# Both FiLM products in one run of matmuls, their 64-row parts in the two row halves of the array, biases added by GpSimd and VectorE

## What is computed

```
Q = x @ Wq ; K = ctx @ Wk                      # 4 heads of 32, 257 context rows of 192
attn = softmax over the 32 largest scores of each row, mean over the heads
c_t  = (attn_mean @ (ctx @ Wv)) * text_mask
x'   = layernorm(x, g_norm_in, b_norm_in)
scale_in, shift_in   = split(c_t @ W_film_in + b_film_in)
x'   = x' * (1 + mod_gate * scale_in) + mod_gate * shift_in
y    = s4d(x')                                 # a causal convolution over the 32 tokens, plus x' * D_skip
scale_out, shift_out = split(c_t @ W_film_out + b_film_out)
y    = y * (1 + mod_gate * scale_out) + mod_gate * shift_out
xt   = x + y ;  xt = xt + gelu(layernorm(xt) @ W1 + b1) @ W2 + b2 ;  layernorm(xt)
```

## Time and profile before

| | |
|---|---|
| median of 3 runs | 705.63 us (705.25 to 710.68) |
| the profiled execution | 706.75 us, its span 705.0 us |
| PE matmul busy | 609.8 us, 87% of the span |
| DVE busy | 524.6 us, 74% |
| ACT busy | 318.5 us, 45% |
| POOL busy | 223.4 us, 32% |

### The profile page before, as it was taken

One profiled execution on the slowest core, in us unless ns is written; L12 is line 12 of the kernel. 1 busy time (PEld: TensorE's weight loads), 2 busy tenths in 40 slices (PEclk: granted clock), 3 DMA queues, 4 the chain that ended last, 5 costly groups with the idle time before them and its releaser, 6 DMA issues.

```text
span 705.0 us, 13818 instructions
## 1 busy us (share of the span) xinstructions
PE 609.8 (87%) x4082; PEld 456.9 (65%) x4082; DVE 524.6 (74%) x1817; ACT 318.5 (45%) x795; POOL 223.4 (32%) x580
## 2 busy tenths in 40 slices
PE   0368377889999999989998999899989999998776
PEld 0134134668787878767877787778777878775665
DVE  5579948486969697968787878788877878885332
ACT  6441011435555555535554555455535454544512
POOL 2540301224242424242524242424242515242420
PEclk9969567999999999999999999999999999999977
DMA  5394040112020303021211212020202030000000
GB/s 161 79 327 134 25 167 24 55 43 75 23 92 14 98 7 104 2 63 42 63 40 32 72 37 66 9 96 8 95 9 96 8 95 9 1 8 1 9 7 8
DMA packets 18462, 40.61 MB, mean 58 GB/s; under 512 B 4741, under 2 KB 11222, under 8 KB 17896
## 3 DMA queue, kind: packets, MB, share of 16 engines
q1 hardware_dynamic: 18408, 40.03, 17.8%
HBM read 37.85 MB, written 2.16 MB: 57 GB/s over the span
## 4 chain that ended last, share of the span: by engine, by line
PE 51%; DVE 30%; issue 10%; ACT 2%; DMA 2%; DVEq 1%; POOL 1%; SPq 1%; POOLq 0%; ACTq 0%
PE D L1067 9%; PE B L1067 6%; PE B L1090 5%; DVE work L835 4%; PE D L1084 4%; PE B L1156 4%; DVE top L829 3%; PE S L1043 3%; PE S L1059 2%; PE S L1060 2%; PE B L1144 2%; PE B L1145 2%; PE PA L1129 2%; DVE ang L862 2%; DVE work L815 2%
## 5 line engine op out<-in xcount | busy, mean ns | idle before, releaser
L485 POOL TENSOR_SCALAR var_in<-mv 128x1 f32<-128x1 f32 x64 | 13.3, 207 | 298.8 <-DVE mv L951 161.8
L835 DVE MATCH_REPLACE8 work<-top,work 128x257 f32<-128x257 f32 x192 | 77.3, 411 | 0.0
L1084 PE MATMUL D<-expw,ang 128*128 128x256 f32 x256 | 71.8, 406 | 5.2 <-ACT ang L550 2.8
L1067 PE MATMUL D<-ang,e_w 128*128 128x128 f32 x512 | 72.5, 289 | 0.0
L829 DVE MAX8 top<-work 128x8 f32<-128x257 f32 x192 | 71.7, 415 | 0.4 <-ACT kern_f L545 0.4
L1067 PEld LDWEIGHTS D<-ang,e_w 128*128 128x128 f32 x512 | 64.5, 199 | 10.1 <-issue 10.1
L1067 PEld LDWEIGHTS B<-ang,w 128*128 128x128 f32 x512 | 60.5, 194 | 7.9 <-issue 6.3
L1067 PE MATMUL B<-ang,w 128*128 128x128 f32 x512 | 60.8, 278 | 0.0
L1090 PE MATMUL B<-expw,ang 128*128 128x256 f32 x256 | 57.9, 379 | 0.0
L1084 PEld LDWEIGHTS D<-expw,ang 128*128 128x128 f32 x256 | 46.5, 196 | 15.9 <-DVE ang L858 6.2
L1090 PEld LDWEIGHTS B<-expw,ang 128*128 128x128 f32 x256 | 47.4, 190 | 5.8
(11 more groups left out here) (244 smaller groups left out, 1277.9 us busy)
## 6 DMA issues: line engine op xcount, KB each, us to landing
ctx_n<-in_ctx_n SPq DMA_DIRECT2D x16, 768.0 KB
ctx_t<-in_ctxT SPq DMA_DIRECT2D x16, 514.0 KB
ctx_t<-in_ctxT SPq DMA_DIRECT2D x16, 257.0 KB
x_all<-in_x SPq DMA_DIRECT2D x4, 512.0 KB, 5.8
out<-out_sb SPq DMA_DIRECT2D x16, 128.0 KB, 1.7
ctx_l<-in_ctx_l SPq DMA_DIRECT2D x64, 24.0 KB
w<-in_W SPq DMA_DIRECT2D x1, 1024.0 KB
e_w<-in_e_w SPq DMA_DIRECT2D x1, 1024.0 KB, 4.8
```

The lines of the kernel that those rows point to most:

```text
L835: V.match_replace(work[:, 2 * q + k, :], top[:, 2 * q + k, 8 * r8:8 * r8 + 8], work[:, 2 * q + k, :], TAKEN).then_inc(chains["taken"], 1)
L1067: ins = MM(bank[:, 128 * m:128 * m + 128], w[:, k, at:at + 128], xs[:, 128 * k:128 * k + 128], start=k == 0, stop=k == 1)
L1084: MM(bank, act2[:, k, :], e_w2[:, k, :], start=True, stop=True).then_inc(s["eo_mm"], 1)
```

## The change

PE computes both ways in one run, ahead of `xf`. `zT2` now has 128 rows: ACT copies the 64-row transpose twice, to rows 0 to 63 and to rows 64 to 127. `film2` is 128 x 512: rows 0 to 63 hold the way in, rows 64 to 127 the way out. The two 64-row matmuls stand one behind the other, in the two row halves of the array, into different banks. The bias row is gone; biases are spread over 128 partitions in `film_b`. For the way in, POOL makes `x_bias = xhat * bias_scale + bias_shift` and DVE adds it to `xf` in a third instruction; for the way out, ACT copies bank B1 to `film_o`, POOL adds the bias, and DVE reads `film_o` in place of the bank. Since the forward transform writes B1, PE waits for that copy (`film_a`). Some semaphores of DVE are joined (`best` into `logit`, `rsd` into `pg`, `pn` into `rsc`) with the same waits.

```diff
@@ loads
-                (brow[64:65, 0:2 * D], d["b_film_in"], "ld_film"), (brow[64:65, 2 * D:4 * D], d["b_film_out"], "ld_film"),
+                (brow[:, 0:2 * D], d["b_film_in"].broadcast_to([128, 2 * D]), "ld_film"), (brow[:, 2 * D:4 * D], d["b_film_out"].broadcast_to([128, 2 * D]), "ld_film"),
@@ GpSimd, step
                 if b:
                     weights(b, 1)
+                if b:
+                    wait_apart(pool, chains["xhat"], b.count(1, 1), passed_g)
+                    wait_apart(pool, s["xf_v"], b.count(1, 0), passed_g)
+                    nc.gpsimd.tensor_tensor(x_bias[:, :], xhat[b.p][:, :], film_b[:, 0:D], ALU.mult).then_inc(chains["xbias"], 1)
+                    wait_apart(pool, chains["xbias"], b.count(1, 1), passed_g)
+                    nc.gpsimd.tensor_tensor(x_bias[:, :], x_bias[:, :], film_b[:, D:2 * D], ALU.add).then_inc(s["xb0_g"], 1)
                 if a:
...
                     norm(2, c)
                 if b:
+                    wait_apart(pool, s["film_a"], b.count(1, 1), passed_g)
+                    nc.gpsimd.tensor_tensor(film_o[:, :], film_o[:, :], film_b[:, 2 * D:4 * D], ALU.add).then_inc(s["film_g"], 1)
                     norm(0, b)
@@ ScalarE, step
                     A(zT1[:, :], PA[:, 256:384], ACT.Copy)
-                    A(zT2[0:64, :], PA[0:64, 384:512], ACT.Copy).then_inc(s["zT_a"], 1)
+                    A(zT2[0:64, :], PA[0:64, 384:512], ACT.Copy)
+                    A(zT2[64:128, :], PA[0:64, 384:512], ACT.Copy).then_inc(s["zT_a"], 1)
+                if b:
+                    wait(act, s["y_mm"], one(b))
+                    wait(act, s["xt_v"], b.count(1, 0))
+                    copy(film_o[:, :], B1[:, :], "film_a")
@@ VectorE, step
                     V.tensor_tensor(xf[:, :], xhat[b.p][:, :], B0[:, 0:D], ALU.mult).then_inc(chains["xf"], 1)
...
-                    V.tensor_tensor(xf[:, :], xf[:, :], B0[:, D:2 * D], ALU.add).then_inc(s["xf_v"], 1)
+                    V.tensor_tensor(xf[:, :], xf[:, :], B0[:, D:2 * D], ALU.add).then_inc(chains["xf"], 1)
+                    wait(dve, chains["xf"], b.count(2, 2))
+                    wait(dve, s["xb0_g"], one(b))
+                    V.tensor_tensor(xf[:, :], xf[:, :], x_bias[:, :], ALU.add).then_inc(s["xf_v"], 1)
...
-                    wait(dve, s["y_mm"], one(b))
-                    V.tensor_tensor(yb[:, :], yb[:, :], B1[:, 0:D], ALU.mult).then_inc(chains["yb"], 1)
+                    wait(dve, s["film_g"], one(b))
+                    V.tensor_tensor(yb[:, :], yb[:, :], film_o[:, 0:D], ALU.mult).then_inc(chains["yb"], 1)
@@ TensorE, step
                     wait(pe, s["gb_a"], b.count(1, 0))
+                    wait(pe, s["xt2_v"], b.count(1, 0))
                     MM(B0[:, :], zT1[:, :], film1[:, 0:512], start=True, stop=False)
-                    MM(B0[:, :], zT2[:, :], film2[:, 0:512], start=False, stop=True).then_inc(s["fin_mm"], 1)
+                    MM(B0[:, :], zT2[0:64, :], film2[0:64, :], start=False, stop=True).then_inc(s["fin_mm"], 1)
+                    MM(B1[:, :], zT2[64:128, :], film2[64:128, :], start=True, stop=False)
+                    MM(B1[:, :], zT1[:, :], film1[:, 512:1024], start=False, stop=True).then_inc(s["y_mm"], 1)
...
                     wait(pe, s["xf_v"], one(b))
-                    wait(pe, s["xt2_v"], b.count(1, 0))
+                    wait(pe, s["film_a"], one(b))
...
-                    MM(B1[:, :], zT1[:, :], film1[:, 512:1024], start=True, stop=False)
-                    MM(B1[:, :], zT2[:, :], film2[:, 512:1024], start=False, stop=True).then_inc(s["y_mm"], 1)
```

More of the change, by code:

```diff
@@ L175, in build @@
         zT1 = sb("zT1", [128, 128])
-        zT2 = sb("zT2", [65, 128])
+        zT2 = sb("zT2", [128, 128])
+        film_o = sb("film_o", [128, 2 * D])
+        x_bias = sb("x_bias", [128, D])
         xf = over("ang", D)
@@ L284, in build @@
         s = {n: sem(n) for n in names}
-        chains = {n: sem("self_" + n) for n in "tm g0 g1 g2 g3 len bn0 bn1 bn2 bn3 top taken u xhat xf logit best pg rsd yb rsc pn pT".split()}
+        chains = {n: sem("self_" + n) for n in "tm xbias g0 g1 g2 g3 len bn0 bn1 bn2 bn3 top taken u xhat xf logit pg yb rsc pT".split()}
         passed_v, passed_g = sem("passed_v"), sem("passed_g")
@@ L887, in step @@
                     V.scalar_tensor_tensor(logit[:, :], dots[:, NE:2 * NE], inorm[:, :], dots[:, 0:NE], ALU.mult, ALU.add).then_inc(chains["logit"], 1)
-                    wait_apart(dve, chains["logit"], one(dd), passed_v)
-                    V.max(best[:, :], logit[:, :]).then_inc(chains["best"], 1)
+                    wait_apart(dve, chains["logit"], dd.count(2, 1), passed_v)
+                    V.max(best[:, :], logit[:, :]).then_inc(chains["logit"], 1)
                 if b:
@@ L897, in step @@
                 if dd:
-                    wait(dve, chains["best"], one(dd))
+                    wait(dve, chains["logit"], dd.count(2, 2))
                     V.tensor_scalar(nbest[:, :], best[:, 0:1], -1.0, None, ALU.mult).then_inc(s["nbest_v"], 1)
@@ L911, in step @@
                     V.scalar_tensor_tensor(pg[:, :], logit[:, :], best[:, 1:2], e_d[:, :], ALU.is_ge, ALU.mult, accum_out=sum_d[:, :]).then_inc(chains["pg"], 1)
-                    wait(dve, chains["pg"], one(dd))
-                    V.reciprocal(rsum_d[:, :], sum_d[:, :]).then_inc(chains["rsd"], 1)
-                    wait(dve, chains["rsd"], one(dd))
+                    wait(dve, chains["pg"], dd.count(2, 1))
+                    V.reciprocal(rsum_d[:, :], sum_d[:, :]).then_inc(chains["pg"], 1)
+                    wait(dve, chains["pg"], dd.count(2, 2))
                     V.tensor_scalar(gate[:, :], pg[:, :], rsum_d[:, :], None, ALU.mult).then_inc(s["gate_v"], 1)
@@ L920, in step @@
                     V.tensor_tensor(xf[:, :], xhat[b.p][:, :], B0[:, 0:D], ALU.mult).then_inc(chains["xf"], 1)
[L921 to L922 removed]
+                    wait(dve, chains["xf"], b.count(2, 1))
+                    V.tensor_tensor(xf[:, :], xf[:, :], B0[:, D:2 * D], ALU.add).then_inc(chains["xf"], 1)
+                    wait(dve, chains["xf"], b.count(2, 2))
+                    wait(dve, s["xb0_g"], one(b))
+                    V.tensor_tensor(xf[:, :], xf[:, :], x_bias[:, :], ALU.add).then_inc(s["xf_v"], 1)
                 if c:
@@ L960, in step @@
                     V.reciprocal(rsum_c[:, :], sum_c[:, :]).then_inc(chains["rsc"], 1)
-                    wait(dve, chains["rsc"], one(c))
-                    V.tensor_scalar(pn_c[:, :], p_c[:, :], rsum_c[:, :], None, ALU.mult).then_inc(chains["pn"], 1)
-                    wait_apart(dve, chains["pn"], one(c), passed_v)
+                    wait(dve, chains["rsc"], c.count(2, 1))
+                    V.tensor_scalar(pn_c[:, :], p_c[:, :], rsum_c[:, :], None, ALU.mult).then_inc(chains["rsc"], 1)
+                    wait_apart(dve, chains["rsc"], c.count(2, 2), passed_v)
                     V.transpose(pT_c[:, :], pn_c[:, :]).then_inc(chains["pT"], 1)
@@ L1233, in _ @@
             pe.wait_ge(s["ld_cent"], LD_CENT)
-            pe.wait_ge(s["fills"], 5)
+            pe.wait_ge(s["fills"], 4)
             def film_products():
                 pe.wait_ge(s["ld_film"], LD_FILM)
-                for rows, m, (f_in, f_out) in ((slice(0, 128), 128, (B0, B1)), (slice(128, 192), 64, (D0, D1))):
-                    for f, bank in enumerate((f_in, f_out)):
-                        for k in range(2):
-                            ins = MM(bank[0:m, :], wvT[:, k, rows], wff[:, k, f * 512:f * 512 + 512], start=k == 0, stop=k == 1)
+                for cols, f, out in ((slice(0, 128), 0, B0[:, :]), (slice(0, 128), 1, B1[:, :]), (slice(128, 192), 0, D0[0:64, :]), (slice(128, 192), 1, D1[64:128, :])):
+                    for k in range(2):
+                        ins = MM(out, wvT[:, k, cols], wff[:, k, f * 512:f * 512 + 512], start=k == 0, stop=k == 1)
                 ins.then_inc(s["film_mm"], 1)
```

34 lines of the change are left out of this document (17 added, 17 removed).

## The result

The changed kernel takes 731.56 us (median of 4 runs, 724.97 to 741.15), the kernel before 705.44 us in the same rounds: ratio 1.0323, interval 1.0223 to 1.0424. It is 3% slower, as forecast (727, range 717 to 741). Set on the chip a second time, it took 726.3 us (725.06 to 733.63). The profiled execution is the longest of the first four, 741.15 us with a span of 739.4, and over 1.5% above the fastest, so its 34 us over the profiled execution of before are more than the usual loss; the trace of the second set (733.63 us, span 731.8) shows the same things and is set beside it where sums are made. Why the runs scatter so much is part of the result: the four of the first set stand in the order of their mean granted clock, from 0.922 at 741.15 us to 0.950 at 724.97.

A forecast was written before the change was run, and what follows sets the result against it. A ring of PE and DVE bounds the kernel. On 706.75 us: 12.6 (14 steps x 0.9), +1.9 (step 1), -0.3 (step 16), 6.2 (copy and POOL), together 20.4, give 727.2; forecast 727 us, range 717 to 741.

The forecast's parts named there:

- the ring: Forward transform, DVE to L858 (10.32 us), PE to the next forward transform (24.7 us): 35.0 us a short step.
- faster, PE is the bound: Rival: PE's work sets the time, so the pair and the `xf` wait save 0.8 us a step: 696 us; chance 0.06.
- Behind the inverse transform the way out is free, ahead of the forward transform it is paid: Removing 1.72 us in DVE's part gains nothing; the new place on PE's part costs +0.9 us a step.
- PE's wait grows to 2 us at L858: At the experts' matmuls L1084, PE's wait for DVE's gated sum grows from about 0.3 to about 2.0 us.
- The pair, 1.06 us: The two 64-row matmuls run side by side: 0.86 us plus 0.2 for switches; bounds 0.86 and 1.92.
- the pair overlaps badly: Rival: only one pass of the pair's four is saved, 734 us, or no overlap, 741 us; chance 0.17.
- Way in to forward transform, 3.76 us: On PE: way in 0.86, pair 1.06, way out 0.86, transpose and scores 0.98; against 2.85 before.
- Short step 36.1, long step 39.4: Sign of being right: forward transforms 36.1 us apart in short steps, 39.4 in long ones.
- copy and POOL: Second `zT2` copy and POOL's delay: 0.2 us a short loop step, 1.1 a long one, 6.2 in all.
- POOL's `x_bias`, 1.1 us in a long step with the copy: POOL's work shifts by about 1.65 us; the way in starts about 1.0 later, 1.1 with the second `zT2` copy.
- `film_a` does not hold the forward transform: ACT's copy of B1 is ready at 3.6 us, under 3.76; if late, it costs 0.1 to 0.3 us.
- Step 16 gives back 0.3: Last step, without search: DVE waits 3.44 us for the way out, which coming earlier gives back 0.3 us.

The follow-up runs named there:

- run 1: Kernel before with both matmuls of the way out left out; 719.77 us beside 706.54, ratio 1.0163.
- run 10: Kernel before with only the second matmul of the way out left out; 705.76 us, ratio 0.9985.
- run 5: Changed kernel with two unused 512-column matmuls added behind the inverse transform; 724.21 us, ratio 1.0238.
- run 6: Changed kernel with the two unused matmuls and POOL's `x_bias` moved behind `norm(1)`; 723.81 us, ratio 1.0246.
- run 8: Changed kernel with two unused 512-column matmuls behind the inverse transform, timed again beside the unedited changed kernel; 723.13 us, ratio 1.0252.
- run 2: Kernel before with only the way out moved ahead of the forward transform, in 65-row form, ACT copying it to `film_o`; 736.64 us, ratio 1.0427.
- run 3: Changed kernel with the last two matmuls exchanged, so the two 64-row ones are no neighbours; 759.11 us, ratio 1.0736.
- run 4: Changed kernel with POOL's two `x_bias` instructions behind `norm(1)` in place of ahead of it; 725.03 us, ratio 1.0239.
- run 7: Changed kernel, unedited, timed again in the same rounds as the one with unused matmuls; 726.3 us, ratio 1.0282.

## Why the prediction held, point by point

It named the sign, the size and the ring, which is the larger part of the mechanism; the clock was not in it. Its account, against three executions that had a trace (spans less the 705.0 us of before):

| part | predicted | after, 739.4 us | after again, 731.8 us | with unused matmuls, 720.7 us |
|---|---|---|---|---|
| start, to the first forward transform | 0 | +2.4 | -0.3 | -0.4 |
| steps 1 and 2 | +3.2 | +5.6 | +4.0 | +2.0 |
| steps 3 to 15 | +17.5 | +28.8 | +27.7 | +16.9 |
| step 16 and the end | -0.3 | -2.4 | -4.5 | -2.8 |
| sum | +20.4 | +34.4 | +26.9 | +15.7 |

- *The ring bounds the kernel, not PE's busy share*: right. Runs 1 and 10 took PE work out and won nothing; runs 5, 6 and 8 added it and lost nothing. The rival "faster, PE is the bound" fell with that.
- *Behind the inverse transform the way out is free, ahead of the forward transform it is paid*: right. Run 2, with little else changed than ACT's copy for it, has short steps of 36.57 against 35.02.
- *PE's wait grows to 2 us at L858*: right in size (1.76), wrong in place: 1.25 of it is the wait for `xln` that comes first, and I had named only the second.
- *The pair, 1.06 us*: right, and the overlap too: first passes start together, 10 ns apart. The 0.2 that I had put on top of 0.86 is there, as 0.1 on each of two passes. The page "TensorE: Matmul & The Clock Gate" of the Trainium skill, Part 3, has matmuls begin in strict program order; the rows show a second pass of L1165 behind the first of L1166, which by program order it precedes, so taken pass by pass that order does not hold here. The rival that the pair overlaps badly fell.
- *Way in to forward transform, 3.76 us*: it is 4.06 in short steps and 4.10 in long ones. This is the term that was mis-sized. I took the neighbours at 0.86 each; the way in took 1.06 and the way out 0.96, 0.3 together. I had put the whole price of the switches, 0.2, on the pair; of the five passes that are 0.1 longer, three are the neighbours'. Runs 2 and 3 show that this belongs to the 64-row form.
- *Short step 36.1, long step 39.4*: 36.37 and 38.67 undisturbed. The short one is 0.3 over, which is the term above: 35.02 + (4.06 - 2.85) + 0.15, by which the way in starts later behind the forward transform than before (32.32 against 32.17 us; 0.2 was predicted for copy and POOL, and with `x_bias` later, run 6, it is 32.3 too).
- *POOL's `x_bias`, 1.1 us in a long step with the copy*: 0.46, by run 4. The shift of `norm(1)` was 1.06 us, not 1.65, and some 0.7 of it was covered. In run 8 the long steps are 1.31 us longer than before in the mean, where I had 2.0; the nine others are 1.3 where I had 1.1. The two errors, some -2.8 and +2.2 us, have opposite signs, which is why 16.9 stands beside 17.5. That the long steps grow by no more than the short ones though POOL's 0.39 is in them has its place in the traces: POOL's weights start 27.59 us behind the forward transform there, in the mean of run 8's four, where before it was 28.00. So 0.4 us was given back ahead of the weights, and -0.41 + 0.47 (weights to way in) + 1.25 (way in to forward transform) is the 1.31. Why that stretch is shorter, no run shows.
- *`film_a` does not hold the forward transform*: right in the loop. In step 16 it did, by 0.67 us.
- *Step 16 gives back 0.3*: it gives back the whole 1.72 us. There is no search in it, PE goes from the inverse transform to the experts without a wait, and the attention of tile `c` (L1227, L1207 before) starts 9.61 us behind the forward transform where it started 11.48 behind. I had looked at DVE's wait for the way out alone.
- *What was not in the account at all*: the granted clock. I had the hole of 2 us in the text and priced it at nothing, because PE has slack there. In the first traced execution nine steps of 3 to 14 lost 0.9 to 1.6 us each to a fall, 11.9 us together (28.8 - 16.9), and steps 1 and 2 stood longer at the lower level; in the second nine steps of 5 to 15 lost 10.8. Both were the longest of their sets. That the median came out at 727.9 is in part luck: if the runs with unused matmuls are taken for after without falls, the account without the clock was 3 us too high by the medians (727 against 723.8) and 5 by the traces (20.4 against 15.7), and the falls filled it.

No version that was tried beats the kernel before with the whole output.

## What to carry to other kernels

Work on an engine that waits anyway may be what keeps it fast: before you move matmuls out of a covered place, look at the hole that they leave and at the granted clock beside it, and price the next microseconds of TensorE at half speed. A float32 matmul of 64 rows in a row half makes its own passes and those of its neighbours some 0.1 us longer here, so that a pair of 512 columns saves 0.36 us and not the 0.86 of a whole matmul, and single ones lose. And where a ring of two engines sets the step, add up what each edit puts on the ring, also at the release next to the one you look at.

## What the runs showed of the hardware

- Less work was slower: 1.72 us of matmuls less a step, 706.5 to 719.8 us in the same rounds (run 1). More unused work did not make the kernel slower: 726.3 to 723.1 us in the same rounds (runs 7 and 8), with the falls gone from steps 3 to 15.
- A fall lasts 3.4 us at clock 0.50 and in the step at 410.86 begins 1.1 us behind the hole (421.26, 422.33); it costs 1.5 us in the short steps, where PE's work stands on the ring, and 0.8 to 1.0 in the long ones. Steps with the same hole and no fall are there too.
- Row halves start together, and a pass of the pair takes 0.53 us (485.37 to 485.90) against 0.43 for a pass of a 512-column matmul on 128 or 65 rows.
- Spacing of matmuls in row halves that are not neighbours: 1.05 us each, also for the 128-row ones between them.
